# Attention and experts in one kernel: layer 0 routes each batch one pass sooner

## The chip, the cores and the metric

The kernel runs as one program on one core of a Trainium2 chip. A core has five engines, each with its own in-order queue: TensorE (PE, with its weight loads as PEld), VectorE (DVE), ScalarE (ACT), GpSimd (POOL) and SyncE (SP); they are held together by semaphores alone. The metric is the device time of one execution in microseconds (us). The kernel before took 808.4 us, the median of three runs (806.72, 808.40, 810.31).

## The reference

32 batches of 128 rows and 128 features pass through two layers; each block adds to the residual `x`. Only layer 0 is touched:

```
x = x + L0_xattn(layernorm(x), ctx, ctx)      # 16 heads of 8
x = x + L0_ffn(layernorm(x))                  # 8 experts, one per row
x = x + L1_xattn(layernorm(x), ctx, mask)     # not touched
x = x + L1_ffn(layernorm(x))                  # not touched

def L0_ffn(inputs):                           # cut to the routing
    num = inputs @ waff.T                     # 8 numbers per row
    aff = num / (norm(inputs) * norm(waff) + 1e-9)
    cap = clip(floor(S * sigmoid(aff.mean() - threshold)), 4, S)
    expert = argmax(aff)                      # "choice"
    keep   = rank of the row in its batch for that expert < cap
    out    = sum over experts of gelu(x_e @ W1_e + b1_e) @ W2_e + b2_e
```

The kernel sorts the rows by expert: it gives each row a place in a table in memory (`sorted_x`), scatters the rows there, and lets the experts work on tiles of 128 sorted rows.

## The kernel before

**Attention and routing interleaved.** Layer 0 runs 32 passes, one per batch `b`. All five engines run the same loop, written out by hand, and each queue's order is the order of the code. In pass `b` TensorE computes scores, exponent shifts, the values product and projections of neighbouring batches. VectorE takes maxima, normalises and makes the new residual of batch `b-1` (`residual`, L735) and, at the end of its pass, its mean and variance (`residual_stats`, L739 and L741, tile `stats`).

**The routing of a batch `r`** is a chain that runs through the passes that follow:
- GpSimd's loop index `r+2`: `route_norm` (L238 to L244) turns the variance into a scale and writes the normalised rows `xn2[r]`, which the trace calls `xy`. From r = 27 (`SCALED`) on, GpSimd only makes the scale and VectorE writes the rows (`route_scale`, L746).
- TensorE in pass `r+4`: `route_transpose` (L336) transposes `xn2[r]`, ScalarE copies it (`route_copy`, L533, tile `r_xnT`), and TensorE multiplies it with `waff` (`affinity`, L367). ScalarE's copy stands in its queue ahead of the pass's four exponentials (L552), which the values product needs.
- VectorE copies the eight numbers (`num_copy`, L628).

**Groups.** Batches are chosen in five groups: 0 to 7, 8 to 15, 16 to 23, 24 to 27 and 28 to 31. For a group GpSimd makes denominators (L253 to L263), VectorE chooses experts in ten small instructions (`choose`, L634 to L673), TensorE counts rows (`places`, L384 to L390) and VectorE turns counts into places (`locate`, L699 to L710, tile `r_pos_s`). Choices of groups 0 and 1 are already spread over five passes (`SPREAD = 2`); group 2 is chosen in one piece in pass 27, group 3 in pass 31, group 4 after the loop.

**Scatter.** GpSimd then sends each batch's rows to their places with one indirect DMA (`scatter`, L270): one in each of the passes 16 to 23, two in 24 to 27, none in 28, up to three from 29 on, and the rest after the loop. GpSimd's queue after the loop is: scale of batch 30, scatter of batch 24 (the first that needs group 3's places), scale of batch 31, denominators of group 4, scatters of batches 25 to 31. The experts' first tile is loaded once all 32 scatters have landed.

**The tail.** After pass 31 come, on TensorE, what is left of the routing (batches 28 to 31, two groups' places), the last output and sums over the experts' weights (`expert_sums_part`, L1003). `LATE = 28` says from which batch on the routing uses PSUM banks that the attention no longer needs.

Of the kernel before, what the change touches and what calls it, by code (L numbers as in the profile page):

```python
# [71 lines left out]
def attention_routing_block(nc, ctx, space, consts, x, ctxT, w, wr, x_res, xn2, stats2, psum, dram):  # L72
# [10 lines left out]
    SPREAD = 2  # L83
# [8 lines left out]
    LATE = 28  # L92
# [220 lines left out]
    def tensor_part(pe, expert_sums_part):  # L313
# [4 lines left out]
        def x_transpose(b, s):  # L318
            pe.wait_ge(xn_ready, b + 1)
            if b == 2:  # L320
                pe.wait_ge(v_ready, 2)
            elif 2 < b < 6:
                pe.wait_ge(qz_ready, b)
            wait(pe, rsem["num"], b - 5)
            nc.tensor.transpose(first_x(b), xn[:, s, :], ident[:]).then_inc(xt_done, 1)

        def route_transpose(r):
            pe.wait_ge(rsem["xn2"], r + 1)
            if r >= LATE:
                pe.wait_ge(mx_ready, 4 * B)  # L330
                pe.wait_ge(rsem["xnT"], r)
            else:
                pe.wait_ge(qz_ready, min(r + 6, B))
            if r == B - 5:
                pe.wait_ge(rsem["num"], r)
            nc.tensor.transpose(xnp[r >= LATE], xn2[:, r, :], ident[:]).then_inc(rsem["xnt"], 1)  # L336
# [23 lines left out]
        def affinity(r):  # L360
            pe.wait_ge(rsem["xnT"], r + 1)
            if r >= LATE:
                pe.wait_ge(mx_ready, 4 * B)
                pe.wait_ge(rsem["num"], r)
            elif r + 4 in close_at:
                pe.wait_ge(rsem["place"], 4 * close_at[r + 4] + 1)
            nc.tensor.matmul(nump[r >= LATE], rt["xnT"][:, r % 2, :], rt["waffT"][:], start=True, stop=True).then_inc(rsem["num_done"], 1)  # L367

        def places(q):
# [5 lines left out]
            if q < SPREAD:  # L375
                pe.wait_ge(rsem["xnT"], z + 4)
            elif z + 5 <= B:
                pe.wait_ge(rsem["xnT"], z + 1)
# [86 lines left out]
        for b in range(B):  # L465
# [4 lines left out]
            if b >= 4:  # L470
                route_transpose(b - 4)
# [4 lines left out]
            else:  # L476
                back_transposes(b - 1, 1 - s)
            minus_max(b, 1)
            if b >= 4:
                affinity(b - 4)  # L480
# [15 lines left out]
            else:  # L496
                route_transpose(B - 4)
        affinity(B - 4)
        back_transposes(B - 1, 1)
        route_transpose(B - 3)  # L500
        places(NG - 2)
# [14 lines left out]
    def scalar_part(act, after_exps):  # L516
# [57 lines left out]
        for b in range(B):  # L574
# [19 lines left out]
            if b >= 3:  # L594
                route_copy(b - 3)
# [5 lines left out]
    def vector_part(dve):  # L601
# [73 lines left out]
        def choose(q):  # L675
            choose_reciprocal(q)
            choose_affinity(q)
            choose_score(q)
            choose_expert(q)
            choose_seen(q)  # L680

# [79 lines left out]
        for b in range(B):  # L761
# [11 lines left out]
            if b >= 4:  # L773
                num_copy(b - 4)
# [7 lines left out]
            if b - 4 in group_at and SPREAD <= group_at[b - 4] < NG - 2:  # L782
                choose(group_at[b - 4])
# [9 lines left out]
            if b == B - 1:  # L793
                residual_stats(b - 1, 1 - s)
                route_scale(b - 2)
                choose(NG - 2)
# [4 lines left out]
        num_copy(B - 4)  # L801
        normalise(B - 1, 1)
        route_scale(B - 2)
        locate(NG - 2)
# [1774 lines left out]
```

## Time and profile before

| | before |
|---|---|
| median of three runs | 808.4 us |
| the profiled execution's own time | 806.13 us |
| its span, first to last instruction | 804.1 us |
| PE busy | 758.8 us, 94% |
| DVE busy | 673.9 us, 84% |
| POOL busy | 477.1 us, 59% |
| ACT busy | 439.8 us, 55% |
| mean granted clock of TensorE | 0.990 of full speed |

Times in the trace are counted from the first instruction. Layer 0 takes the time to about 218 us, the experts come next, and layer 1 follows. Shares of the whole span say little about the stage that the change touches: each stretch is to be read by itself. An idle time in brackets behind an instruction is that of its engine just before it, with the instruction that ended it. The changed kernel's line numbers are those of before up to about L500, then one less, and from about L680 on five more.

### The profile page before, as it was taken

To read this page: it belongs to the slowest core of one execution; us is meant where nothing else is said; L and a number is where in the kernel's file an instruction comes from. 1 tells how busy PE (TensorE), PEld (TensorE's weight loads), DVE (VectorE), ACT (ScalarE), POOL (GpSimd) and SP (SyncE) were. 2 spreads that over 40 slices of the span, in tenths; PEclk is the share of its full clock that TensorE was granted. 3 is DMA by queue.
4 is the path that set the end of the run, shared out by engine and by line. 5 is a ranking of instruction groups with operands and counts; after the bars stand their busy time and mean duration, and the time that the engine had idled before them with its cause. 6 is when DMAs were issued, how large, how long until landed. Compare 5 with 4: busy or idle time off the path is not lost.

```text
span 804.1 us, 28859 instructions
## 1 busy us (share of the span) xinstructions
PE 758.8 (94%) x10843; PEld 639.3 (80%) x10873; DVE 673.9 (84%) x1776; ACT 439.8 (55%) x1077; POOL 477.1 (59%) x914
## 2 busy tenths in 40 slices
PE   8999999998789999899999999999999999999973
PEld 6777777766689997788888888888888888888861
DVE  5888889887767765599999999999899999999876
ACT  3666666656066663545555555655545555555442
POOL 6758578888768664244654655646546555464334
PEclk9999999999999999999999999999999999999996
DMA  8986320000422211121131221221322313213120
GB/s 239 369 344 236 146 84 15 19 15 29 145 74 63 61 47 37 39 65 45 44 87 45 61 73 46 81 52 46 87 46 60 73 45 76 57 46 78 39 44 14
DMA packets 68253, 65.81 MB, mean 82 GB/s; under 512 B 23714, under 2 KB 49042, under 8 KB 68114
## 3 DMA queue, kind: packets, MB, share of 16 engines
q1 hardware_dynamic: 53250, 39.71, 18.6%
q10 hardware_dynamic: 12816, 20.06, 6.7%
q0 software_dynamic: 2048, 4.20, 1.8%
q8 instruction: 86, 1.41, 0.7%
q14 instruction: 53, 0.43, 0.2%
HBM read 35.89 MB, written 24.37 MB: 75 GB/s over the span
## 4 chain that ended last, share of the span: by engine, by line
PE 55%; DVE 19%; DMA 12%; issue 5%; SPq 4%; POOL 3%; ACT 1%; DVEq 1%; ACTq 0%; another core or an unknown queue 0%; POOLq 0%
DMA a_r_all<-a_r_rows 6%; DMA a_r_rows<-a_rT 4%; PE psum L432 4%; PE psum L1932 4%; PE psum L1042 4%; PE psum L1816 4%; PE psum L1864 4%; SPq L1481 3%; PE psum L1832 3%; PE psum L421 3%; PE psum L1845 3%; PE psum L1898 3%; PE psum L414 3%; PE psum L1030 3%; DVE a_mxf L2273 2%
## 5 line engine op out<-in xcount | busy, mean ns | idle before, releaser
L2114 ACT ACTIVATE a_pT<-psum 128x512 f32<-128x512 f32 x128 | 69.5, 594 | 49.0 <-PE psum L1919 34.0
L720 DVE TENSOR_REDUCE l_mx<-psum 128x4 bf16<-128x512 f32 x128 | 81.9, 682 | 3.5 <-PE psum L403 1.8
L1587 POOL TENSOR_TENSOR f_hd<-f_hmc,a_wmean 128x1 f32<-128x1 f32 x32 | 6.7, 210 | 130.1 <-DVE f_hr L2373 128.8
L2273 DVE TENSOR_REDUCE a_mxf<-psum 128x8 f32<-128x1024 f32 x64 | 77.5, 1211 | 3.1 <-PE psum L1888 3.1
L1832 PEld LDWEIGHTS psum<-a_cTm,a_Wk 128*128 128x128 f32 x512 | 64.2, 191 | 19.6 <-issue 19.6
L1816 PEld LDWEIGHTS psum<-a_xT,a_Wq 128*128 128x128 f32 x512 | 64.3, 192 | 14.2 <-issue 13.4
L552 ACT ACTIVATE l_pT<-psum 128x512 f32<-128x512 f32 x128 | 70.5, 597 | 7.8 <-PE psum L421 7.5
L1581 POOL TENSOR_SCALAR f_hq<-f_ht 128x512 bf16<-128x512 f32 x31 | 60.3, 1946 | 20.0 <-ACT f_ht L2158 19.9
L1898 PE MATMUL psum<-a_qT,a_kT 64*128 64x128 f32 x1024 | 71.0, 278 | 0.0
L1832 PE MATMUL psum<-a_cTm,a_Wk 128*128 128x128 f32 x512 | 70.1, 281 | 0.0
L1864 PE MATMUL psum<-a_Wv,a_cTm 128*128 128x512 f32 x128 | 69.8, 632 | 0.1
L1816 PE MATMUL psum<-a_xT,a_Wq 128*128 128x128 f32 x512 | 69.6, 279 | 0.0
L2158 ACT ACTIVATE f_ht<-f_h,f_big_m,f_hr 128x512 f32<-128x512 f32 x32 | 26.0, 814 | 77.6 <-DVE f_hr L2373 75.5
L1932 PE MATMUL psum<-a_pT,a_v 128*32 128x128 f32 x2048 | 62.7, 274 | 0.6 <-DVE a_oT L2298 0.6
L1845 PE MATMUL psum<-a_Wo,a_oT 128*128 128x128 f32 x512 | 62.6, 275 | 0.0
L1898 PEld LDWEIGHTS psum<-a_qT,a_kT 64*128 64x128 f32 x1024 | 62.1, 188 | 0.0
L1932 PEld LDWEIGHTS psum<-a_pT,a_v 128*32 128x32 f32 x2048 | 53.9, 110 | 8.7 <-issue 5.9
L1845 PEld LDWEIGHTS psum<-a_Wo,a_oT 128*128 128x128 f32 x512 | 59.7, 192 | 0.2 <-issue 0.2
L421 PEld LDWEIGHTS psum<-negI,l_mx 128*128 128x128 bf16 x512 | 34.9, 100 | 25.0 <-DVE l_mx L720 22.7
L2145 ACT COPY a_v<-psum 128x512 f32<-128x512 f32 x64 | 37.6, 588 | 21.3 <-PE psum L1864 21.3
L1103 ACT ACTIVATE e_hT<-psum,e_w1t 128x128 f32<-128x128 f32 x156 | 44.6, 369 | 6.4 <-issue 5.7
L2298 DVE TENSOR_TENSOR a_oT<-psum,a_r_all 128x512 f32<-128x512 f32 x64 | 41.7, 678 | 7.1 <-issue 4.5
(322 smaller groups left out, 2064.1 us busy)
## 6 DMA issues: line engine op xcount, KB each, us to landing
sorted_x<-r_zeros ACTq DMA_DIRECT2D x12, 1408.0 KB, 7.0
a_r_all<-a_r_rows SPq DMA_DIRECT2D x124, 128.0 KB
e_xt<-sorted_x SPq DMA_DIRECT2D x39, 64.0 KB, 1.8
sorted_y<-e_yt ACTq DMA_DIRECT2D x39, 64.0 KB, 1.6
e_w<-in_E_W1b SPq DMA_DIRECT2D x1, 2064.0 KB
a_cin<-in_ctx SPq DMA_DIRECT2D x32, 64.0 KB, 2.7
out<-f_x SPq DMA_DIRECT2D x32, 64.0 KB, 2.3
x_res<-in_x SPq DMA_DIRECT2D x1, 512.0 KB, 5.2
```

The source lines that it names most:

```text
L421: last = nc.tensor.matmul(tp[k][:, j * S:(j + 1) * S], mx[:, b % 2, h:h + 1].to_broadcast([P, P]), negI[:], start=False, stop=(j == Q4 - 1 ...
L552: nc.scalar.activation(pT[:, k, :], tp[k], ACT.Exp, scale=SCALE).then_inc(exp_ready, 1)
L720: nc.vector.tensor_reduce(mx[:, s, Q4 * k:Q4 * k + Q4], maxp[k % 2].rearrange("p (h t) -> p h t", h=Q4), AX_X, ALU.max).then_inc(mx_ready, 1)
L1581: nc.gpsimd.tensor_scalar(hq[:], ht[:], -M, 127.0, ALU.add, ALU.min).then_inc(hq_ready, 1)
L1816: last = nc.tensor.matmul(bank[:, i * S:(i + 1) * S], Wq[:, 4 * half + i, :], xT[:, b % 2, :], start=True, stop=True)
L1832: last = nc.tensor.matmul(bank[:, i * S:(i + 1) * S], Wk[:, 4 * half + i, :], context_of(b), start=True, stop=True)
L1845: last = nc.tensor.matmul(pa[:, 0:D], oT[:, p, :], Wo[:, p, :], start=(p == 0), stop=(p == NP - 1))
L1864: nc.tensor.matmul(bank, context_of(b), Wv[:, 512 * half:512 * half + 512], start=True, stop=True).then_inc(v_done, 1)
L1898: last = nc.tensor.matmul(tp[e][:, i * S:(i + 1) * S], keys_of(b)[r, p, :], qT[r, b % 2, p, :], start=(half == 0 and i == 0), stop=(half = ...
L1932: last = nc.tensor.matmul(op[half][32 * j:32 * j + 32, i * S:(i + 1) * S], values_of(b)[:, 8 * half + 4 * e + i, part], pT[:, 2 * half + e ...
L2114: nc.scalar.activation(pT[:, 2 * half + e, :], tp[e], ACT.Exp, scale=SCALE).then_inc(exp_ready, 1)
L2273: nc.vector.tensor_reduce(mxf[:, 8 * half:8 * half + 8].rearrange("p (e h) -> p e h", e=2), psum[:, 0:2, :].rearrange("p e (h t) -> p e h ...
```

## The change

Only layer 0's schedule changes. The arithmetic and the number of instructions on TensorE, VectorE and GpSimd stay as they are.
- `route_transpose`, `affinity`, `route_copy` and `num_copy` of batch `r` move from pass `r+4` to pass `r+3`. In passes 30 and 31, where VectorE writes the rows, the transpose stands behind the back transposes of the attention instead of ahead of them.
- Batch 28 is routed in pass 31, no longer after the loop, and `LATE` is 29.
- The choice of groups 2 and 3 is cut in two: `choose_first` (five instructions) in passes 26 and 30, `choose_second` (five) in passes 27 and 31.
- After the loop, group 3's counting stands first on TensorE, and its `locate` first on VectorE.

GpSimd's code is not changed.

```diff
-    LATE = 28
+    LATE = 29
...
-            wait(pe, rsem["num"], b - 5)
+            wait(pe, rsem["num"], b - 4)
             nc.tensor.transpose(first_x(b), xn[:, s, :], ident[:]).then_inc(xt_done, 1)
...
-                pe.wait_ge(qz_ready, min(r + 6, B))
-            if r == B - 5:
+                pe.wait_ge(qz_ready, min(r + 5, B))
+            if r >= B - 5:
                 pe.wait_ge(rsem["num"], r)
...
-            elif r + 4 in close_at:
-                pe.wait_ge(rsem["place"], 4 * close_at[r + 4] + 1)
+            elif r + 3 in close_at:
+                pe.wait_ge(rsem["place"], 4 * close_at[r + 3] + 1)
...
             if q < SPREAD:
-                pe.wait_ge(rsem["xnT"], z + 4)
+                pe.wait_ge(rsem["xnT"], z + 5)
             elif z + 5 <= B:
-                pe.wait_ge(rsem["xnT"], z + 1)
+                pe.wait_ge(rsem["xnT"], z + 2)
...
-            if b >= 4:
-                route_transpose(b - 4)
+            if 3 <= b < SCALED + 3:
+                route_transpose(b - 3)
             if b in close_at:
                 places(close_at[b])
             if b == 0:
                 expert_sums()
             else:
                 back_transposes(b - 1, 1 - s)
+            if b >= SCALED + 3:
+                route_transpose(b - 3)
             minus_max(b, 1)
-            if b >= 4:
-                affinity(b - 4)
+            if b >= 3:
+                affinity(b - 3)
...
-            else:
-                route_transpose(B - 4)
-        affinity(B - 4)
+        places(NG - 2)
         back_transposes(B - 1, 1)
         route_transpose(B - 3)
-        places(NG - 2)
         affinity(B - 3)
...
             pv_copy(b, s)
-            if b >= 3:
-                route_copy(b - 3)
+            if 2 <= b < B - 1:
+                route_copy(b - 2)
...
-        def choose(q):
+        def choose_first(q):
             choose_reciprocal(q)
             choose_affinity(q)
             choose_score(q)
+
+        def choose_second(q):
             choose_expert(q)
             choose_seen(q)
...
-            if b >= 4:
-                num_copy(b - 4)
+            if b >= 3:
+                num_copy(b - 3)
...
-            if b - 4 in group_at and SPREAD <= group_at[b - 4] < NG - 2:
-                choose(group_at[b - 4])
+            if b - 3 in group_at and SPREAD <= group_at[b - 3] < NG - 1:
+                choose_first(group_at[b - 3])
+            if b - 4 in group_at and SPREAD <= group_at[b - 4] < NG - 1:
+                choose_second(group_at[b - 4])
...
                 residual_stats(b - 1, 1 - s)
                 route_scale(b - 2)
-                choose(NG - 2)
...
-        num_copy(B - 4)
+        locate(NG - 2)
         normalise(B - 1, 1)
         route_scale(B - 2)
-        locate(NG - 2)
         num_copy(B - 3)
```

On VectorE, the choice of group 2 in pass 27 of the kernel before, from the residual to the next batch's queries (`l_qz`); `r_` tiles are the routing's:

```order
L735 TENSOR_TENSOR x_res<-psum,l_xb 128x128
L634 RECIPROCAL r_tmp<-r_den 128x64
L642 TENSOR_TENSOR r_aff<-r_num,r_tmp 128x64
L644 TENSOR_REDUCE r_mval<-r_aff 128x8
L651 TENSOR_TENSOR r_tmp<-r_aff,r_mval 128x64
L654 TENSOR_TENSOR r_score<-r_tmp,r_weight 128x64
L661 TENSOR_REDUCE r_smax<-r_score 128x8
L663 TENSOR_TENSOR r_tcrb<-r_score,r_smax 128x64
L669 TENSOR_TENSOR r_tcr<-r_score,r_smax 128x64
L671 TENSOR_REDUCE r_gsum<-r_tcr 128x8
L673 TENSOR_TENSOR r_seen<-r_seen,r_gsum 128x8
L622 SCALAR_TENSOR_TENSOR l_qz<-psum,l_bq,group_rows 128x512
```

The same place of VectorE in the changed kernel, now in pass 26:

```order
L740 TENSOR_TENSOR x_res<-psum,l_xb 128x128
L633 RECIPROCAL r_tmp<-r_den 128x64
L641 TENSOR_TENSOR r_aff<-r_num,r_tmp 128x64
L643 TENSOR_REDUCE r_mval<-r_aff 128x8
L650 TENSOR_TENSOR r_tmp<-r_aff,r_mval 128x64
L653 TENSOR_TENSOR r_score<-r_tmp,r_weight 128x64
L621 SCALAR_TENSOR_TENSOR l_qz<-psum,l_bq,group_rows 128x512
```

The other five instructions stand at the same place of pass 27, between `x_res` and `l_qz`; group 3 is cut in the same way in passes 30 and 31.

On TensorE, from the values product of pass 31 (L432) into the tail, in the kernel before; L336 and L367 are routing, L385 to L390 group 3's places, L439 and L444 the attention's last transposes:

```order
L432 MATMUL psum<-l_pT,l_v 32x128 x16
L336 MATMUL psum<-ident,xy 128x128
L367 MATMUL psum<-r_waffT,r_xnT 128x8
L439 MATMUL psum<-ident,l_oev 128x128 x4
L336 MATMUL psum<-ident,xy 128x128
L385 MATMUL psum<-r_tcrb,r_before_t 128x32
L388 MATMUL psum<-r_tcrb,r_ones_b 128x24
L388 MATMUL psum<-r_tcrb,r_ones_b 128x16
L388 MATMUL psum<-r_tcrb,r_ones_b 128x8
L390 MATMUL psum<-r_seen,r_ones_b 128x32
L367 MATMUL psum<-r_waffT,r_xnT 128x8
L444 MATMUL psum<-ident,l_on 128x128
```

The same stretch of TensorE in the changed kernel:

```order
L432 MATMUL psum<-l_pT,l_v 32x128 x16
L385 MATMUL psum<-r_tcrb,r_before_t 128x32
L388 MATMUL psum<-r_tcrb,r_ones_b 128x24
L388 MATMUL psum<-r_tcrb,r_ones_b 128x16
L388 MATMUL psum<-r_tcrb,r_ones_b 128x8
L390 MATMUL psum<-r_seen,r_ones_b 128x32
L439 MATMUL psum<-ident,l_oev 128x128 x4
L336 MATMUL psum<-ident,xy 128x128
L367 MATMUL psum<-r_waffT,r_xnT 128x8
L444 MATMUL psum<-ident,l_on 128x128
```

One transpose and one affinity (batch 28) are gone from between the values product and the back transposes, and the places stand in front.

On TensorE in pass 31, around the first and second exponent shifts (L421), in the kernel before:

```order
L414 MATMUL psum<-l_qz,l_kT 128x512 x4
L421 MATMUL psum<-negI,l_mx 128x128 x4
L336 MATMUL psum<-ident,xy 128x128
L439 MATMUL psum<-ident,l_oev 128x128 x4
L421 MATMUL psum<-negI,l_mx 128x128 x4
L367 MATMUL psum<-r_waffT,r_xnT 128x8
```

The same in the changed kernel; pass 30 reads alike:

```order
L414 MATMUL psum<-l_qz,l_kT 128x512 x4
L421 MATMUL psum<-negI,l_mx 128x128 x4
L439 MATMUL psum<-ident,l_oev 128x128 x4
L336 MATMUL psum<-ident,xy 128x128
L421 MATMUL psum<-negI,l_mx 128x128 x4
L367 MATMUL psum<-r_waffT,r_xnT 128x8
```

The transpose, now of batch 28 instead of 27, has moved behind the back transposes.

## Rows read from the trace of the kernel before

**Rows 1.** Windows, passes 25 and 28: us, engines' busy time, clock, DMA share, GB/s.

```profile
156.11:161.87 5.76, 5.74 (x90) 4.44 (x90) 4.81 (x13) 3.81 (x10) 4.95 (x8) 1.00 0.07 23
173.38:181.59 8.21, 6.34 (x98) 4.74 (x98) 7.49 (x25) 3.89 (x10) 7.13 (x11) 1.00 0.05 16
```

**Rows 2.** Waits of POOL, 153.6 to 218.1 us: total us, times, longest.

```profile
POOL r_vpe L238 <- DVE stats L741: 0.5, 1, 0.5
```

**Rows 3.** Timeline of POOL in the tail: start us, length, line, tiles, [idle before].

```profile
204.43 1.08 POOL L270 DMA_INDIRECT sorted_x<-xy,r_pos_s  x1 [1.42 <-DVE r_pos_s L710]
205.55 0.25 POOL L238 TENSOR_SCALAR r_vpe<-stats 128x1 f32<-128x1 f32 x1
```

**Rows 4.** Timeline of DVE, the statistics of batch 31.

```profile
204.77 0.18 DVE L741 BATCH_NORM_AGGREGATE stats<-l_bn 128x2 f32<-128x6 f32 x1
```

**Rows 5.** Timeline of PE, the route transposes of passes 27, 28 and 29.

```profile
170.12 0.28 PE L336 MATMUL psum<-ident,xy 128*128 128x128 f32 x1
...
176.97 0.30 PE L336 MATMUL psum<-ident,xy 128*128 128x128 f32 x1 [0.93 <-DVE l_qz L622]
...
184.09 0.28 PE L336 MATMUL psum<-ident,xy 128*128 128x128 f32 x1
```

**Rows 6.** Timeline of POOL, normalised rows of batches 24 to 26, scale of 27.

```profile
171.21 0.81 POOL L244 TENSOR_SCALAR xy<-x_res,stats,r_rs 128x128 f32<-128x128 f32 x1
...
177.76 0.81 POOL L244 TENSOR_SCALAR xy<-x_res,stats,r_rs 128x128 f32<-128x128 f32 x1
...
184.30 0.81 POOL L244 TENSOR_SCALAR xy<-x_res,stats,r_rs 128x128 f32<-128x128 f32 x1
...
185.52 0.22 POOL L238 TENSOR_SCALAR r_vpe<-stats 128x1 f32<-128x1 f32 x1
```

**Rows 7.** Timeline of DVE, passes 26 and 27: queries, and the choice of group 2.

```profile
168.26 0.75 DVE L622 SCALAR_TENSOR_TENSOR l_qz<-psum,l_bq,group_rows 128x512 f32<-128x512 f32 x1 [0.69 <-PE psum L351]
...
173.24 0.55 DVE L634 RECIPROCAL r_tmp<-r_den 128x64 f32<-128x64 f32 x1
...
176.09 0.74 DVE L622 SCALAR_TENSOR_TENSOR l_qz<-psum,l_bq,group_rows 128x512 f32<-128x512 f32 x1
```

**Rows 8.** Timeline of DVE: statistics of batch 27, rows of batch 27.

```profile
184.57 0.18 DVE L741 BATCH_NORM_AGGREGATE stats<-l_bn 128x2 f32<-128x6 f32 x1
...
190.34 0.33 DVE L746 TENSOR_SCALAR xy<-x_res,stats,r_rs 128x128 f32<-128x128 f32 x1
```

**Rows 9.** Timeline of POOL beside the choice of group 2: a scatter.

```profile
173.96 1.07 POOL L270 DMA_INDIRECT sorted_x<-xy,r_pos_s  x1 [0.17 <-issue]
```

**Rows 10.** Timeline of PE, the route transpose of pass 30.

```profile
189.76 0.28 PE L336 MATMUL psum<-ident,xy 128*128 128x128 f32 x1
```

**Rows 11.** Timeline of ACT: copy of a transpose in pass 30; last attention copy.

```profile
190.08 0.27 ACT L533 COPY r_xnT<-psum 128x128 f32<-128x128 f32 x1 [1.08 <-PE psum L336]
...
199.86 0.57 ACT L557 COPY l_oev<-psum 128x512 f32<-128x512 f32 x1
```

**Rows 12.** Timeline of PE, back transposes of batch 31.

```profile
200.89 0.63 PE L439 MATMUL psum<-ident,l_oev 128*128 128x128 f32 x4
```

**Rows 13.** Timeline of DVE: residual of batch 30, normalisation and residual of batch 31.

```profile
197.95 0.29 DVE L735 TENSOR_TENSOR x_res<-psum,l_xb 128x128 f32<-128x128 f32 x1 [1.19 <-PE psum L450]
...
202.00 0.25 DVE L726 RECIPROCAL l_rden<-psum 128x16 f32<-128x16 f32 x1
...
204.12 0.28 DVE L735 TENSOR_TENSOR x_res<-psum,l_xb 128x128 f32<-128x128 f32 x1
```

**Rows 14.** Windows, columns as in rows 1: the kernel's end, the start of the experts.

```profile
788.00:792.00 4.00, 0.86 (x3) 0.22 (x3) 3.62 (x14) 1.77 (x3) 1.84 (x6) 0.59 0.00 0
218.10:223.43 5.33, 2.71 (x7) 0.90 (x5) 5.26 (x6) 0.27 (x1) 5.33 (x6) 1.00 0.13 40
```

**Rows 15.** Groups by line on PE, 785 to 804.1 us: busy us, mean ns.

```profile
L1981 PE MATMUL psum<-f_wq,f_xqT 128*128 128x512 bf16 x2 | 1.1, 545 | 0.0
```

**Rows 16.** The same group of PE, 400 to 785 us.

```profile
L1981 PE MATMUL psum<-f_wq,f_xqT 128*128 128x512 bf16 x27 | 10.2, 379 | 0.8 <-ACT a_v L2145 0.7 <-issue 0.2
```

More of the change, by code:

```diff
@@ L678, in choose @@
             choose_score(q)
+        def choose_second(q):
             choose_expert(q)
             choose_seen(q)
+        def choose(q):
+            choose_first(q)
+            choose_second(q)
         def choose_spread(q, part):
```

## The prediction

> **What bounds the kernel now.** I read the shares of the engines first, then the windows of layer 0, then who waits in its last third, and last the timelines of that third. Over the whole span TensorE is nearly always busy, and so it is in layer 0's loop: a pass takes 5.76 us and holds 5.74 us of matmuls [rows 1]. The reader should stop at the second of these windows. Pass 28 takes 8.21 us with 6.34 of matmuls, so something else decides there.
>
> Two engines share the last third. GpSimd, at 59% of the span an unlikely candidate, has almost no rest from 153.6 us to the end of its scatters at about 218: the table of its waits has one of 0.5 us on statistics [rows 2] and one of 1.42 us, in the tail, ahead of the scatter of batch 24, which stood ready and waited for group 3's places [rows 3]. From 205.55 on, where it scales batch 31, it only works off its own queue: denominators, then seven scatters; nothing that TensorE or VectorE do later than the statistics of batch 31 ends that chain. So the end of layer 0 is the start of that one instruction (L238 at 205.55) plus a fixed rest, and every edit is to be priced by what it does to that start. It has two possible releasers: GpSimd's own queue, which decided before, and the statistics of batch 31, ready at 204.77 + 0.18 = 204.95 [rows 4].
>
> **Passes 3 to 26.** Transpose, copy, affinity and number copy are the same instructions one batch on, at the same place of the pass. They cost nothing as long as the rows of batch r are there a pass sooner. GpSimd's rows are early while it scatters at most once a pass; I take the cost as nothing. The same instructions no longer follow the values product of pass 31.
>
> **Pass 27: a new wait.** From pass 24 on GpSimd scatters twice a pass and falls behind. In pass 27 TensorE's L336 started at 170.12 [rows 5] with batch 23; now batch 24 stands there, whose rows GpSimd finishes at 171.21 + 0.81 = 172.02 [rows 6]. TensorE waits 1.90 us. Behind it in TensorE's queue stand the back transposes and the rest of the pass, and ScalarE's copy stands ahead of the exponentials, so the whole pass moves by 1.90; GpSimd doesn't, since it works off a backlog.
>
> **Passes 28 and 29.** Batch 25 is ready at 177.76 + 0.81 = 178.57, against 176.97 before: 1.60 late. The wait isn't added to the one before, since the releaser is the same GpSimd, which kept its times. The 0.93 us that TensorE waited there for `l_qz` [rows 5] are swallowed by it. Batch 26 is ready at 185.11, and TensorE now comes at 184.09 + 1.60 = 185.69: no wait. Delay so far 1.60.
>
> The split of the choice doesn't pay beyond that. It took 176.09 - 173.24 = 2.85 us in pass 27 [rows 7] and held `l_qz` and with it the transpose of pass 28. Half of it now lies in pass 26, where VectorE rested 0.69 us ahead of `l_qz` [rows 7]; some 0.8 us stick out and end in pass 27, beside the 1.90 us for which TensorE waits for GpSimd. The other half falls under the wait in pass 28. If that cover went, the 0.8 would be paid.
>
> GpSimd itself is now held once: it scaled batch 27 at 185.52 [rows 6] and its statistics were ready at 184.57 + 0.18 = 184.75 [rows 8]; 1.60 later is 186.35, so it waits 0.83 us. That is less than the 1.42 us of rest that it had in the tail.
>
> The first half of the choice now runs ahead of GpSimd's rows of batch 24 instead of behind them. The trace has a scatter beside the choice with 1.07 us [rows 9], and one in the tail with 1.08 [rows 3]: no sign that the one slows the other, so I take nothing. The Trainium skill, "SBUF — State Buffer", section "Who interferes with whom", says that a VectorE instruction with two inputs in SBUF and a GpSimd instruction that reads SBUF take turns. By that page three such instructions of about 0.2 us each could make batch 24 some 0.6 us later, and the forecast would be about 0.6 us higher; the scatter's two rows speak against it.
>
> **Passes 30 and 31.** Here VectorE writes the rows at the end of its pass. Those of batch 27 are done at 190.34 + 0.33 = 190.67 [rows 8], and L336 of pass 30 started at 189.76 [rows 10]: 0.91 us too early. ScalarE's copy (at 190.08, 0.32 after L336 [rows 11]) is late by the same, and the exponentials behind it too; the back transposes that now go first fill TensorE's wait, not ScalarE's. Both ends: nothing if the back transposes (0.63 [rows 12]) covered TensorE and ScalarE's own slack the rest, 1.2 with the copy's 0.27 on top. I take 0.91, the difference of the two rows, for each of the two passes. Delay at the residual of batch 30: 1.60 + 2 x 0.91 = 3.42 us, 197.95 [rows 13] becomes 201.37. Group 3's first half lies in VectorE's wait of pass 30, the second (under 2.85 / 2 = 1.4 us) behind that residual while TensorE does the values product, so it only delays the scale of batch 30, which has room.
>
> **The tail.** Before, the back transposes of batch 31 started at 200.89 [rows 12], behind batch 28's affinity. That is gone, and what is late next is ScalarE's copy, done at 199.86 + 0.57 = 200.43 [rows 11]; + 3.42 gives 203.85, so they are 2.96 late. Before, VectorE took them up at 202.00 [rows 13] though they were done at 200.89 + 0.63 = 201.52, since the choice of group 3 and a number copy stood ahead. Those 0.48 us are gained: the group's places are found while ScalarE still copies. 2.96 - 0.48 = 2.48, so the statistics of batch 31 come at 204.95 + 2.48 = 207.43. The residual at 204.12 [rows 13] stood behind four small instructions of `locate`, which may give another 0.3; I leave it.
>
> GpSimd by itself would be there sooner. The scatter of batch 24 needs no wait of 1.42 any more, but it lost 0.83: 205.55 + 0.83 - 1.42 = 204.96. So the statistics decide: the scale of batch 31 starts at 207.43 instead of 205.55, **1.9 us later**, with GpSimd resting some 2.5 us ahead of it. All behind it keeps its distances, as group 4's choice follows GpSimd's denominators. The experts and layer 1 have the same code and start 1.9 us later.
>
> Against the profiled execution's own 806.13 us that is 808.0. The median of the three runs is 2.3 us above that execution, so on the scale of the runs it is 808.4 + 1.9 = **810.3**. That is 0.2%. A measurement of this kernel can tell about 0.5%, 4 us, from no change, so the forecast is no change that shows, on the slow side. With the bounds above (passes 30 and 31 between 0 and 1.2 each, 0.3 in the tail, 0.6 for the port) the mechanism itself gives 810.3 - 2.1 = 808.2 to 810.3 + 1.2 = 811.5.
>
> **Rivals.** *The tail gains and nothing is lost (807.0).* If TensorE reached batch 31 without the new waits, its statistics would come at 204.95 - 0.94 (the 3.42 - 2.48 that the tail saves) = 204.01, ahead of GpSimd, which then closes its whole rest of 1.42 us: 808.4 - 1.4. More can't be won, since GpSimd has no other rest. For it: the 1.42 us are real, and what pass 28 lost (8.21 - 5.76) is larger than any one new wait. Against it: rows 5 and 6 hold the transposes to GpSimd's times, whatever else is faster.
>
> *The waits add up (813.2, slower).* This takes GpSimd being held by TensorE already in passes 27 and 28, so that its rows keep their distance behind. Then the price is 1.90 in pass 27, 1.60 in 28, 185.11 - 184.09 = 1.02 in 29 and 0.91 twice, 6.34, less 0.94 in the tail: statistics at 204.95 + 5.40 = 210.35, 4.8 us after 205.55, and 808.4 + 4.8. It decides from the point where statistics come later than GpSimd asks for them. In pass 29 that is 0.77 us away [rows 6, 8], for it; in the passes before, GpSimd has a backlog and asked late [rows 2], against it.
>
> *TensorE's clock falls (820).* The new waits give TensorE rests of up to 1.9 us. The granted clock is 1.00 (2.4 GHz) in a window with only 2.71 us of matmuls in 5.33, and 0.59 in one with 0.86 in 4.00 [rows 14]; passes 27 to 31 hold 5.7 in some 7.7, so by the rows it stays. If it fell to 1.2 GHz, a 512-column matmul takes 545 ns [rows 15] instead of 379 [rows 16], 44% more: 5.74 x 0.44 = 2.5 us a pass, 10 for the four that follow. The Trainium skill, "TensorE: Matmul & The Clock Gate", section "Part 1: The HAM clock gate", says that the clock of a TensorE that rests is halved until it has worked again. By that page alone a longer rest would bring this rival about; this trace agrees for the kernel's end and shows none in layer 0.
>
> **How the numbers follow.** Forecast 0.72, gain 0.17, adding up 0.08, clock 0.03. The three runs lie from 1.7 below to 1.9 above their median. The low end is the gain's 807.0 less 1.7, the high end the forecast's own upper bound, 811.5, plus 1.9: 805.3 to 813.4, which also holds the middle of the waits that add up. Faster by over 0.5% (under 804.4) takes the gain and more luck than the three runs show: 0.04. Slower by over 0.5% (over 812.4) has the clock, more than half of the adding up, and a high run of the forecast: 0.12. The rest, 0.84, is no change.
>
> **What would show it.** In the trace of the changed kernel: L336 of pass 27 idle some 1.9 us ahead of it with GpSimd's L244 as releaser, L336 of pass 28 at about 178.6, and that of 29 without a wait; one wait of GpSimd for statistics near 186; about half a microsecond at L336 of passes 30 and 31 with VectorE's `xy` as releaser and ScalarE's copy 0.9 late; no wait of a scatter for `r_pos_s` in the tail, but one of about 2 us of L238 for the statistics of batch 31; last scatter's end near 220. Wrong would be: transposes of passes 27 and 28 that don't wait, batch 31 scaled before 205.5, GpSimd's rows of batches 24 and 25 moved by more than 0.3 us, or a difference that arises behind the experts' first tile.

## The result and the profile after

The changed kernel takes 810.77 us, the kernel before 808.14 us, medians of 22 runs each; the ratio is 1.0033 with a 95% interval of 1.0017 to 1.0048. That is +2.6 us: slower, and by less than the 0.5% that the prediction called "no change". The profiled execution of the changed kernel has a span of 806.7 us (before 804.1).

Single runs lie up to some 5 us to either side of their median, so I read the stage that the change touches by itself. I take it from the start of the values product (L432) of pass 25 to the end of the last scatter: 56.21 us before (161.87 to 218.08), 60.62 us after (160.89 to 221.51), 4.4 us more. Windows of the changed kernel, one for each of the passes 26 to 31, then the tail up to GpSimd's scale of batch 31, then the rest up to the last scatter. Columns as in [rows 1]; the last three are granted clock, DMA share and GB/s.

```profile
160.89:166.65 5.76, 5.75 (x90) 4.44 (x90) 4.86 (x14) 3.81 (x10) 4.84 (x10) 1.00 0.01 3
166.65:176.29 9.64, 7.84 (x89) 6.20 (x89) 6.97 (x22) 4.03 (x10) 8.25 (x14) 0.77 0.09 29
176.29:184.72 8.43, 7.23 (x100) 5.49 (x99) 5.82 (x17) 3.90 (x10) 6.96 (x12) 0.86 0.05 16
184.72:190.38 5.66, 5.66 (x90) 4.42 (x89) 4.51 (x11) 3.80 (x11) 2.42 (x5) 1.00 0.02 6
190.38:196.82 6.44, 5.49 (x83) 3.69 (x82) 4.81 (x13) 3.74 (x10) 5.04 (x9) 1.00 0.10 33
196.82:203.38 6.56, 5.14 (x74) 3.38 (x74) 4.14 (x15) 2.96 (x8) 5.31 (x7) 1.00 0.09 30
203.38:209.00 5.62, 4.08 (x58) 3.35 (x59) 3.72 (x19) 2.85 (x7) 2.92 (x5) 1.00 0.12 38
209.00:221.51 12.51, 9.95 (x86) 9.17 (x85) 8.42 (x37) 0.27 (x1) 9.79 (x14) 1.00 0.73 207
```

Read it by differences from before, whose lengths in the same order were 5.75, 5.76, 8.21, 5.68, 5.52, 5.50, 7.26 and 12.53: pass 27 loses 3.88, pass 28 0.22, passes 30 and 31 0.92 and 1.06, the tail gives back 1.64. The second thing to see is the clock: 0.77 and 0.86 in passes 27 and 28, where the kernel before had 1.00.

TensorE's route transposes of passes 27 to 31, which answer to [rows 5, 10]:

```profile
171.10 0.33 PE L336 MATMUL psum<-ident,xy 128*128 128x128 f32 x1 [1.79 <-POOL xy L244]
179.85 0.28 PE L336 MATMUL psum<-ident,xy 128*128 128x128 f32 x1
187.21 0.28 PE L336 MATMUL psum<-ident,xy 128*128 128x128 f32 x1
193.84 0.33 PE L336 MATMUL psum<-ident,xy 128*128 128x128 f32 x1 [0.36 <-DVE xy L751]
200.68 0.33 PE L336 MATMUL psum<-ident,xy 128*128 128x128 f32 x1 [0.75 <-DVE xy L751]
```

GpSimd, to be held against [rows 2, 3, 6]: the rows of batch 25, the scale of batch 27, the scatter of batch 24, the scale of batch 31.

```profile
176.78 0.81 POOL L244 TENSOR_SCALAR xy<-x_res,stats,r_rs 128x128 f32<-128x128 f32 x1
...
187.96 0.23 POOL L238 TENSOR_SCALAR r_vpe<-stats 128x1 f32<-128x1 f32 x1 [2.91 <-DVE stats L746]
...
205.90 1.08 POOL L270 DMA_INDIRECT sorted_x<-xy,r_pos_s  x1 [0.25 <-DVE r_pos_s L715]
...
209.00 0.22 POOL L238 TENSOR_SCALAR r_vpe<-stats 128x1 f32<-128x1 f32 x1 [2.02 <-DVE stats L746]
```

GpSimd kept its times: the rows of batch 25 are done 16.70 us after the start of the stage in both kernels. The scatter's wait of 1.42 us is gone, and GpSimd rests 2.02 us for the statistics of batch 31 instead, as forecast. What was not forecast starts at 171, in windows of one microsecond of the same kernel:

```profile
169.00:170.00 1.00, 0.30 (x4) 0.13 (x3) 1.00 (x3) 0.00 (x0) 0.83 (x3) 1.00 0.25 82
170.00:171.00 1.00, 0.00 (x0) 0.00 (x0) 0.32 (x2) 0.00 (x0) 0.89 (x2) 1.00 0.00 0
171.00:172.00 1.00, 0.90 (x10) 0.89 (x10) 0.10 (x1) 0.54 (x2) 0.81 (x4) 0.91 0.00 0
172.00:173.00 1.00, 1.00 (x12) 0.79 (x10) 0.84 (x5) 0.82 (x2) 0.82 (x2) 0.50 0.00 0
...
178.00:179.00 1.00, 1.00 (x21) 0.70 (x16) 0.20 (x1) 0.58 (x1) 0.89 (x2) 0.67 0.00 0
```

TensorE (first busy column) rests from 169.3 to 171.1, and just after it has started again the granted clock falls to 0.50, the level of 1.2 GHz, and stays there to about 178.7 although TensorE is busy throughout.

### The profile page after: what moved, and what is told of

Its sections match the earlier page's. It is cut to its first block, busy times and chain, and to the rows that moved or that the text cites. A ratio compares the mean times of both kernels' runs of the same rounds, so it can differ in the third digit from the quotient of the medians.

```text
span 806.7 us, 28891 instructions
## 1 busy us (share of the span) xinstructions
PE 765.1 (95%) x10873; PEld 640.5 (79%) x10873; DVE 673.6 (84%) x1776; ACT 439.8 (55%) x1077; POOL 477.0 (59%) x914
## 3 DMA queue, kind: packets, MB, share of 16 engines
q8 instruction: 86, 1.41, 0.7%
## 4 chain that ended last, share of the span: by engine, by line
PE 55%; DVE 19%; DMA 12%; issue 5%; SPq 4%; POOL 4%; ACT 1%; DVEq 1%; ACTq 0%; POOLq 0%
DMA a_r_all<-a_r_rows 6%; PE psum L1047 4%; PE psum L1937 4%; DMA a_r_rows<-a_rT 4%; PE psum L1821 4%; PE psum L432 4%; PE psum L1837 4%; SPq L1486 4%; PE psum L1869 4%; PE psum L1850 3%; PE psum L1035 3%; PE psum L1903 3%; PE psum L421 3%; PE psum L414 3%; DVE a_mxf L2278 2%
## 5 line engine op out<-in xcount | busy, mean ns | idle before, releaser
L421 PEld LDWEIGHTS psum<-negI,l_mx 128*128 128x128 bf16 x512 | 35.4, 100 | 25.0 <-DVE l_mx L725 23.5
```

Of the source, the lines that this page charges most:

```text
L421: last = nc.tensor.matmul(tp[k][:, j * S:(j + 1) * S], mx[:, b % 2, h:h + 1].to_broadcast([P, P]), negI[:], start=False, stop=(j == Q4 - 1 ...
```

## The experiments

The theory after the result: the doubled scatters ahead of batch 24's rows make TensorE wait 1.8 us in pass 27; that rest lets the clock fall; passes 30 and 31 lose by VectorE's late rows. The rivals: the loss is the wait alone, the clock's fall is chance, or it comes from elsewhere (the halved choice, the experts).

**1. Even scatters: take away what makes TensorE wait.**

```diff
-            for _ in range(1 if b < 24 else 2 if b < 29 else 3):
+            for _ in range(1 if b < 26 else 2 if b < 29 else 3):
```

> The changed kernel, with GpSimd's scatters spread otherwise: one a pass up to pass 25, two in 26 to 28, three after (before: two in 24 to 27, none in 28). The same scatters in all, so by pass 29 GpSimd is where it was. Theory (late rows of batch 24 in pass 27 cost a wait, and the wait costs TensorE's clock): rows of batch 24 come some 2.5 us sooner, L336 of passes 27 and 28 doesn't wait, the granted clock stays 1.00 there, and the time falls by 1.9 + 2.1 = 4.0 us against the changed kernel, so it is 806 to 807.5, at or under the kernel before. Rival (the loss is in passes 30 and 31 and the tail, and the wait of pass 27 is only taken from a later one): under 1 us better than the changed kernel, 810.

Measured: ratio to before 0.9982 (0.9951 to 1.0013). Passes 27 and 28 and the last scatters of this kernel:

```profile
166.22:172.32 6.10, 5.80 (x89) 4.43 (x89) 5.86 (x19) 3.81 (x10) 5.15 (x9) 1.00 0.07 24
172.32:179.75 7.43, 6.37 (x98) 4.75 (x98) 6.13 (x20) 3.89 (x10) 6.52 (x11) 1.00 0.05 18
...
203.70:216.21 12.51, 10.94 (x89) 9.65 (x88) 8.42 (x37) 0.27 (x1) 9.79 (x14) 1.00 0.82 213
```

The wait in pass 27 is gone, the clock stays at 1.00, and the two passes take 13.53 us instead of 18.07, the stage 55.75 instead of 60.62. So the doubled scatters are the origin of what passes 27 and 28 lose, 4.54 of the 4.87 us. Passes 30 and 31 stay long (6.44 and 6.20). The ratio is 0.5%, 4.1 us, under the changed kernel's, as the theory wanted; experiment 10 finds half of that.

**2. Keep the wait, fill the rest.** TensorE multiplies the identity with itself while GpSimd's rows are on their way.

```diff
+            if b == 27:
+                pe.wait_ge(oev_ready, b)
+                for _ in range(14):
+                    nc.tensor.matmul(yp[:, 0:S], ident[:], ident[:], start=True, stop=True)
             if 3 <= b < SCALED + 3:
```

> The changed kernel with 14 matmuls of ident with ident in pass 27 ahead of the route transpose, into a bank that the next transposes overwrite (their result is used by nothing): TensorE works while it waits. Theory (the clock falls because TensorE rests): the transpose starts as late as in the changed kernel, within 0.2 us, but the clock stays 1.00 in passes 27 and 28, and the time falls by about 2 us against the changed kernel, to some 808.7. Rival (the clock fell in the one profiled execution only, or for another reason): the time stays at 810.8, and the clock falls here too or fell in no other execution.

Measured: ratio 1.0036 (1.0004 to 1.0067), stage 58.66 us. Passes 27 and 28:

```profile
166.16:175.09 8.93, 8.91 (x117) 7.61 (x118) 5.98 (x19) 3.81 (x10) 7.63 (x12) 1.00 0.07 24
175.09:182.26 7.17, 6.16 (x98) 4.71 (x99) 6.10 (x20) 3.90 (x10) 6.21 (x12) 1.00 0.09 29
```

The fillers run over: the transpose starts 5.67 us into the pass, after 4.45 in the changed kernel, so the wait even grew by 1.22 us. Yet the clock stays at 1.00 and the two passes take 16.10 us instead of 18.07. So some 2.0 us of the loss are the clock's, at the least, if it is the fillers that kept it: this is one execution, while in all the other profiles with that wait the clock fell in pass 27 or 28. Without it the two passes take between 14.88 (16.10 - 1.22) and 16.10, an estimate of 0.9 to 2.1 us over before's 13.97; the forecast said 1.60. The theory's 2 us didn't show in the whole time (1.0036, the changed kernel 1.0033): behind the last scatter this execution took 590.1 us, the changed kernel 585.2.

**3. GpSimd writes the rows of batches 27 and 28 too.**

```diff
-    SCALED = 27
+    SCALED = 29
```

> The changed kernel with SCALED = 29: GpSimd writes the rows of batches 27 and 28 as well, VectorE those of 29 to 31 only, and the transposes of passes 30 and 31 stand ahead of the back transposes again. Theory (passes 30 and 31 lose 0.9 to 1.1 us each since VectorE writes the rows too late): both waits for VectorE's xy go, passes 30 and 31 take some 5.6 us instead of 6.5, GpSimd's 2 x 0.81 us more lie in its rests; 1.5 to 2 us better than the changed kernel, 809. Rival (GpSimd is the bound in the tail): the two rows make it 1.6 us later there, 810.8 or more.

Measured: ratio 1.0002 (0.9976 to 1.0028), stage 59.53 us. TensorE waits 1.78 us in pass 27. Passes 30, 31 and the two parts of the tail:

```profile
188.48:194.00 5.52, 5.06 (x83) 3.67 (x82) 4.56 (x12) 3.72 (x10) 4.27 (x7) 1.00 0.08 27
194.00:199.77 5.77, 4.99 (x74) 3.48 (x75) 3.64 (x14) 3.08 (x8) 4.68 (x8) 1.00 0.07 23
199.77:206.76 6.99, 4.45 (x51) 3.27 (x52) 4.10 (x19) 2.90 (x7) 6.05 (x9) 0.78 0.12 40
206.76:220.29 13.53, 12.48 (x92) 11.70 (x92) 7.83 (x36) 0.27 (x1) 9.70 (x15) 0.86 0.72 201
```

Passes 30 and 31 are 0.92 and 0.79 us shorter than in the changed kernel: VectorE's rows made them long. Passes 27 and 28 keep the same wait, and the clock falls there again (16.28 us together). But the gain doesn't reach the end: the tail takes 20.52 us instead of 18.13, with the clock down. GpSimd scaled batch 31 without a wait, so its own queue was the bound there, as the rival said.

**4. The wait alone, in the kernel before.**

```diff
+            if b == 27:
+                pe.wait_ge(rsem["xn2"], 25)
             if b >= 4:
                 route_transpose(b - 4)
```

> The kernel before with one wait more and nothing else: TensorE in pass 27 waits for the rows of batch 24, as the changed kernel does, though it transposes batch 23. Theory (this one wait and the clock after it make the loss): L336 of pass 27 starts some 1.9 us late, the clock falls to 0.50 for 5 to 7 us behind it, TensorE is 2.5 to 3 us late in pass 29, and the statistics of batch 31 come so much later than GpSimd wants them: 809.5 to 811, as slow as the changed kernel. Rival (GpSimd's 1.42 us of rest and pass 28's 2.4 us of slack hide it): 808.1, no change.

Measured: ratio 1.0016 (0.9991 to 1.0042), stage 60.17 us. The transpose of pass 27, then passes 27 and 28:

```profile
170.27 0.33 PE L336 MATMUL psum<-ident,xy 128*128 128x128 f32 x1 [1.79 <-POOL xy L244]
```

```profile
165.83:173.59 7.76, 5.96 (x90) 4.47 (x90) 4.87 (x14) 3.81 (x10) 6.48 (x11) 1.00 0.06 19
173.59:183.45 9.86, 7.85 (x99) 6.09 (x99) 7.63 (x25) 4.04 (x10) 8.76 (x15) 0.83 0.09 28
```

One wait of 1.79 us put into the kernel before costs its stage 3.96 us against the first profile of before. Of these, 2.00 are the wait's, in pass 27 at full clock. The clock falls in pass 28, behind a second rest (1.08 us, `l_qz`), and that pass takes 9.86 us instead of 8.21. It falls once more in the tail, and the last part takes 0.93 us more:

```profile
206.78:220.24 13.46, 12.43 (x90) 11.63 (x89) 7.83 (x36) 0.27 (x1) 9.72 (x15) 0.85 0.67 202
```

Such falls come without the added wait too. The second profile of the kernel before (experiment 9) has as much time at half clock in its stage, 10.2 us by windows of a quarter microsecond, though not all in the same places; against that one the wait costs 60.17 - 58.27 = 1.90 us. The whole time decides nothing here: its interval holds both the theory's loss and the rival's "no change".

**5. Even scatters and GpSimd's rows together**, the candidate that should have beaten both: the edits of 1 and 3.

> The changed kernel with the scatters held to one a pass until pass 26 (as in the experiment with even scatters) and, besides, GpSimd writing the normalised rows of batches 27 and 28 as well (SCALED = 29). Theory (each wait of TensorE in passes 27, 30 and 31 has its own releaser, and two edits remove them all): passes 27 to 31 take about 6.1, 7.4, 5.7, 5.5 and 5.6 us, against 6.10, 7.43, 5.69, 6.44 and 6.20 with even scatters alone; if the tail keeps its 5.6 + 12.5 us, the last scatter ends 54.2 us after the values of pass 25, 2.0 us before the kernel before (56.2), and the ratio of the times is 0.995 to 0.999. Rival (the rows written on GpSimd only push its scatters into the tail, and TensorE's clock falls there as it did when the rows alone were moved): the tail takes 20 to 20.5 us instead of 18.1, the stage ends at 56.2 and the ratio is 0.999 to 1.002.

Measured: ratio 1.0012 (0.9989 to 1.0034), stage 57.34 us. Passes 27 to 30 are as hoped (6.10, 7.43, 5.67, 5.52), but pass 31 takes 8.42 at a clock of 0.80. TensorE and GpSimd there:

```profile
195.64 0.33 PE L336 MATMUL psum<-ident,xy 128*128 128x128 f32 x1 [1.76 <-POOL xy L244]
```

```profile
192.25 0.96 POOL L270 DMA_INDIRECT sorted_x<-xy,r_pos_s  x1 [0.30 <-issue]
...
194.77 0.81 POOL L244 TENSOR_SCALAR xy<-x_res,stats,r_rs 128x128 f32<-128x128 f32 x1
```

Neither theory held: three scatters (at 189.56, 190.98 and 192.25) stand ahead of batch 28's rows, and the wait of pass 27 has come back four passes later, clock included.

**6. Even scatters, the choice whole again.**

```diff
-                choose_first(group_at[b - 3])
...
-                choose_second(group_at[b - 4])
+                choose(group_at[b - 4])
```

> The changed kernel with even scatters, and the choice of the third and fourth group whole in one pass again (four passes behind, as in the kernel before), not halved. Theory (the halving moves work that VectorE has room for): every pass within 0.3 us of the run with even scatters, the last scatter at 55.75 +- 0.5 us after the values of pass 25. Rival (the halving pays, since with routing a pass sooner VectorE's queue is full in the pass in which a group closes): pass 28, where the whole choice then stands, is 0.8 us longer or more (8.2 against 7.4) and the end is later by as much.

Measured: ratio 1.0014 (0.9990 to 1.0037), stage 58.73 us. Passes 27 and 28 take 5.75 and 8.37, together 14.12 us against 13.53 in experiment 1: the halving pays 0.59 us. Pass 28 alone is 0.94 us longer, as the rival said, and its transpose shows why:

```profile
175.81 0.30 PE L336 MATMUL psum<-ident,xy 128*128 128x128 f32 x1 [1.09 <-DVE l_qz L621]
```

The tail up to the scale of batch 31 takes 6.57 us instead of 5.62, at a clock of 0.84.

**7. Even scatters in the kernel before.** The edit of 1 with 26 in place of 24, nothing else.

> The kernel before with the scatters held to one a pass until pass 26, nothing else. Theory (in the kernel before GpSimd's rows are asked for a pass later and its doubled scatters of passes 24 and 25 lie under that slack): passes 27 to 31 within 0.2 us of the kernel before (5.76, 8.21, 5.68, 5.52, 5.50), the end within 0.3 us of 56.2 but for what the clock does in the tail, ratio 1.000 +- 0.002. Rival (even scatters are worth something by themselves, so that the gain of the changed kernel with even scatters is not the change's): pass 28 drops from 8.21 to 7.4, the end to 55.4 or sooner, ratio 0.998 or less.

Measured: ratio 0.9997 (0.9976 to 1.0019), stage 57.44 us. Pass 27 takes 5.76, pass 28 9.42 at a clock of 0.82. So even scatters by themselves show no gain, neither in pass 27 nor in the time. The surprise is the clock: TensorE waits in pass 28 for the same tile as in the kernel before (1.07 us for `l_qz`, before 0.93), and this time the clock fell, there and in the tail.

**8. The changed kernel again, twice, unaltered.**

> The changed kernel, unaltered, once more with a profile on another chip. Theory (the wait of 1.8 us in pass 27 is what takes TensorE's clock down, and does so whenever the kernel runs): TensorE waits 1.7 to 1.9 us for GpSimd's rows in pass 27, the granted clock of pass 27 is 0.75 to 0.9, and passes 27 and 28 together take 17.5 to 18.5 us. Rival (the fall of the clock was a chance of that one execution): the same wait, a clock of 1.00, and passes 27 and 28 together take 16.0 to 16.4 us.

> The changed kernel, unaltered, a third time. Theory (the wait for GpSimd's rows in pass 27 is the same in every execution, the fall of the clock that follows is not): TensorE waits 1.75 to 1.9 us in pass 27; the stage takes 58 to 58.4 us if the clock stays at 1.00 in all passes and 59.5 to 60.8 us if it falls in pass 27 or 28. Rival (the clock falls in every execution of this order): it falls in pass 27 or 28 here too.

Measured: stages of 59.67 and 59.56 us. TensorE waited 1.83 and 1.79 us in pass 27, but that pass kept its full clock both times; the clock fell in pass 28. Passes 27 and 28 of the third execution (the second: 7.79 and 9.31), then its transpose of pass 28:

```profile
165.81:173.57 7.76, 5.95 (x90) 4.48 (x90) 5.97 (x19) 3.81 (x10) 6.48 (x11) 1.00 0.06 19
173.57:182.81 9.24, 7.81 (x99) 6.09 (x99) 6.00 (x20) 4.03 (x10) 8.14 (x14) 0.82 0.09 30
```

```profile
176.79 0.33 PE L336 MATMUL psum<-ident,xy 128*128 128x128 f32 x1 [0.57 <-POOL xy L244]
```

Their sums, 17.10 and 17.00, are under the 17.5 that the theory allowed and over the rival's 16.4. The clock fell in all three executions, as the rival of the second repeat said, but not in the same place. The transpose shows what the first profile hid: where pass 27 keeps its clock, TensorE comes to pass 28 early enough to wait for GpSimd again, as forecast.

**9. The kernel before again, unaltered.**

> The kernel before, unaltered, once more with a profile on another chip. Theory (whether a rest of TensorE of 1 to 2 us is followed by half clock differs from one execution to the next, and the kernel before has such rests in pass 28 and in the tail): TensorE waits in the same places for the same lengths within 0.2 us, but the clock falls in pass 28 or in the tail, and the stage takes 57 to 58 us instead of 56.2. Rival (its rests are too short for that): clock 1.00 in all of these passes and in the tail to the scale of batch 31, 56.2 +- 0.3 us.

Measured: a stage of 58.27 us, 2.06 more than in the first profile. TensorE's waits in pass 28 first, of the first profile and of this one:

```profile
176.97 0.30 PE L336 MATMUL psum<-ident,xy 128*128 128x128 f32 x1 [0.93 <-DVE l_qz L622]
177.83 0.19 PE L385 MATMUL psum<-r_tcrb,r_before_t 128*128 128x64 bf16 x1 [0.56 <-ACT r_xnT L533]
```

```profile
175.03 0.30 PE L336 MATMUL psum<-ident,xy 128*128 128x128 f32 x1 [0.95 <-DVE l_qz L622]
175.89 0.19 PE L385 MATMUL psum<-r_tcrb,r_before_t 128*128 128x64 bf16 x1 [0.56 <-ACT r_xnT L533]
```

And the windows around them, again the first profile and then this one:

```profile
176.00:177.00 1.00, 0.07 (x2) 0.06 (x1) 1.00 (x3) 0.00 (x0) 0.97 (x3) 1.00 0.16 57
177.00:178.00 1.00, 0.44 (x8) 0.28 (x9) 1.00 (x3) 0.69 (x2) 0.81 (x2) 1.00 0.03 8
178.00:179.00 1.00, 1.00 (x19) 0.99 (x15) 0.90 (x6) 0.12 (x2) 0.92 (x3) 1.00 0.00 0
```

```profile
174.00:175.00 1.00, 0.09 (x2) 0.00 (x0) 1.00 (x3) 0.00 (x0) 0.98 (x3) 1.00 0.12 41
175.00:176.00 1.00, 0.41 (x6) 0.28 (x7) 1.00 (x2) 0.63 (x2) 0.81 (x3) 1.00 0.08 25
176.00:177.00 1.00, 1.00 (x19) 0.99 (x17) 0.90 (x6) 0.14 (x1) 0.92 (x3) 0.94 0.00 0
177.00:178.00 1.00, 0.96 (x11) 0.68 (x11) 0.93 (x6) 0.60 (x1) 0.89 (x2) 0.50 0.00 0
...
182.00:183.00 1.00, 1.00 (x24) 0.59 (x12) 0.62 (x1) 0.00 (x0) 0.89 (x2) 0.50 0.00 0
```

The same program, the same waits to 0.02 us, nearly the same busy shares, and once the clock stays at 1.00, once it is 0.50 from 177 to 183 and again for 3.4 us in the tail. So the profile on which the prediction rests showed the lucky one of two outcomes.

**10. Even scatters again**, to see whether they beat the kernel before.

> The changed kernel with even scatters once more, on another chip, since the first comparison (0.9982, 0.9951 to 1.0013) left open whether it beats the kernel before. Theory (the stage is 0.5 to 2 us shorter than the kernel before, the more so where TensorE's clock falls in that kernel and not here): the last scatter 55.5 to 56.0 us after the values of pass 25, clock 1.00 throughout, ratio 0.997 to 0.9995. Rival (the first look was a lucky execution, and the clock falls in the tail here too, as in the run with the whole choice): the stage takes 57 us or more, ratio 1.000 to 1.002.

Measured: ratio 1.0008 (0.9991 to 1.0026), stage 55.73 us, each pass within 0.02 us of experiment 1. They don't: the two ratios lie on both sides of 1. Weighted by their intervals they make 1.0002 +- 0.0015, an estimate; the changed kernel's 1.0033 +- 0.0016 lies 0.0031 +- 0.0022 above it. So holding the scatters back takes the loss out of the time as well, and gains nothing beyond it. The stage is the shortest of all, 0.5 to 2.5 us shorter than the kernel before, and the time doesn't show it.

**11. The changed kernel with the choice whole**, its scatters as they are (the edit of 6).

> The changed kernel with its doubled scatters from pass 24 as they are, and the choice of the third and fourth group whole again. Theory of the prediction (TensorE is late in pass 28 by GpSimd's rows in any case, so that the halving pays nothing): passes 27 and 28 together within 0.5 us of the changed kernel at like clock, which is 15.4 to 16.4 us where the granted clock stays 1.00 and 17 to 18.1 us where it falls. Rival (it pays as it did beside even scatters, 0.6 us, because VectorE's late quotient l_qz is one more wait): TensorE waits some 1 us for l_qz in pass 28, and the two passes take 0.6 us or more beyond that.

Measured: stage 61.91 us. Passes 27 and 28 and the tail up to the scale of batch 31:

```profile
166.41:176.18 9.77, 7.98 (x89) 6.34 (x90) 5.86 (x16) 4.03 (x10) 8.39 (x14) 0.76 0.09 29
176.18:184.54 8.36, 7.09 (x99) 5.36 (x99) 7.10 (x23) 3.89 (x10) 6.89 (x12) 0.87 0.05 18
...
203.21:209.88 6.67, 5.20 (x53) 4.09 (x54) 4.73 (x24) 2.85 (x7) 2.90 (x5) 0.68 0.10 32
```

The two passes take 18.13 us, the changed kernel 18.07 with the clock down in the same place: under GpSimd's rows the halving pays nothing, as the prediction said, and the transpose of pass 28 waits for nothing. But the tail takes 1.05 us more, as it took 0.95 more in experiment 6. How much of that is the choice of group 3 and how much the clock (0.68 and 0.84) isn't separated.

**Where the rest of the time goes.** From the last scatter to the end the kernel before takes 586.0 and 588.3 us in its two profiles, the changed kernel 585.2, 585.4 and 585.4, even scatters 590.9 and 588.2; over all fourteen profiles it is 584.8 to 591.2. So what a stage gains can be lost behind it. In experiment 10 the clock fell right behind the last scatter, as the experts' first tile began, and was 0.50 from 222 to 225:

```profile
222.00:223.00 1.00, 1.00 (x7) 1.00 (x6) 1.00 (x2) 0.00 (x0) 0.11 (x1) 0.50 0.24 66
```

In layer 1 VectorE's exponent shifts (`a_mx`) are late more often: from 312 to 785 us TensorE waits for them 3 times in the changed kernel's first profile, 1.3 us in all, and 8 times, 3.1 us, in experiment 1. It does so 3 and 6 times in the two profiles of before, 4 and 3 times in the repeats of the changed kernel, 7 times in experiment 10. Why layer 1, whose code is the same, falls into one or the other stays open; no run was made for it.

## Why the prediction was right, and where not

- **The result.** +1.9 us was forecast, 2.6 us measured (1.4 to 3.9 by the interval), in the likeliest case. That the two lie so near is in part luck: the forecast left out the clock, which fell in all three profiles of the changed kernel and in one of the two of before, and it left out the spread of the parts behind the stage. At a clock of 1.00 in both kernels, experiment 2 puts the changed stage between 57.44 (58.66 - 1.22) and 58.66 us, an estimate of 1.2 to 2.5 us over before's 56.21; the 1.9 lies in it.
- **The wait of pass 27**: 1.90 forecast, 1.79, 1.83 and 1.79 measured in three executions, with the releaser named. Experiment 4 puts the same wait into the kernel before and finds 2.00 us in the pass; experiment 1 takes its origin away. The 0.6 us allowed for the port were not paid: GpSimd's rows of batch 24 are done 10.15 us after the start of the stage in both kernels.
- **Passes 27 and 28 together**: +1.60 forecast, because the second wait isn't added and swallows that for `l_qz`. The repeats, in which pass 27 kept its clock, bear this out up to the transpose of pass 28, which comes 16.79 and 16.75 us after the start of the stage, before 15.10: 1.69 and 1.65 late, by GpSimd's rows. For both passes without the clock the estimate is +0.9 to +2.1 (experiment 2). With it, +4.10, +3.13 and +3.03 against the first profile of before. The term had the right mechanism and left out the clock.
- **Passes 30 and 31**: 0.91 each forecast, 0.92 and 1.06 measured, and experiment 3 shows the cause. TensorE's part is the wait of 0.36 and 0.75. ScalarE's copy, which stands ahead of the exponentials, comes 1.02 and 1.41 us later in its pass than before, and the exponentials start right behind it:

```profile
194.21 0.27 ACT L532 COPY r_xnT<-psum 128x128 f32<-128x128 f32 x1 [2.09 <-PE psum L336]
...
201.04 0.27 ACT L532 COPY r_xnT<-psum 128x128 f32<-128x128 f32 x1 [2.49 <-PE psum L336]
```

- **The tail**: the delay of 3.42 at the residual of batch 30 was to become 1.9 at the scale of batch 31, 1.5 given back; measured 1.64. GpSimd rests 2.02 ahead of it (2.5 forecast) and no longer for `r_pos_s` of group 3 (1.42 before, 0.25 after). "All behind it keeps its distances" held here (12.53 before, 12.51 after), but not where the clock fell in the tail: in experiment 3 that part takes 13.53 us, as one of its scatters waits 1.41 us for group 4's places.
- **GpSimd held in pass 29**: 0.83 forecast, 2.91 measured in the first profile and 2.36 in the third. The step is right and its input, the delay of 1.60, was too small: pass 28 ended 4.11 and 3.05 us late, the clock's part included.
- **"The split of the choice doesn't pay beyond that"**: right under the cover that was named (experiment 11), and 0.59 us where the cover is gone (experiment 6), against the 0.8 forecast for that case. In the tail the prediction took 0.48 us for VectorE's earlier choice of group 3. With the choice whole the tail is 1.05 and 0.95 us longer, but the fallen clock comes with it in both experiments, so what the split is worth there stays open.
- **The step that failed**, though the time came out in the range, is "so by the rows it stays", of the clock, with a chance of 0.03. The row that I leaned on, 1.00 with 2.71 us of work in 5.33 [rows 14], was one outcome of several. The price was too high as well: in passes 27 and 28 the clock was down for 3.4 to 6.8 us and cost some 2 us where it was longest (experiment 2), not 10. The two profiles of the kernel before differ in whether it falls at all. The Trainium skill, "TensorE: Matmul & The Clock Gate", section "Part 1: The HAM clock gate", says that the window by which the clock is set runs free and doesn't start anew with a kernel, so that the point at which the clock rises varies from run to run. It says so of the rise alone; the profiles here show that a fall varies too (1.00 and 0.50 behind the same waits in experiment 9).
- **"The experts and layer 1 ... start 1.9 us later"** and else the same: not so. What lies behind the last scatter varies by up to 2.7 us between executions of one kernel, which no row of one profile could show, and it was 0.6 to 3.1 us shorter in the changed kernel's three profiles than in the two of before. That is a difference behind the experts' first tile, one of the prediction's own signs of being wrong; whether it comes of the change or of chance stays open.

With all clocks as they fell, the changed kernel's three stages have a mean of 59.95 us, the two of before 57.24: a difference of 2.7 us. That it is so near to the 2.6 us of the medians shows little: the same five executions differ by only 0.5 us in their whole time (means of 807.8 and 807.4 us), since the parts behind the stage vary by as much.

## What to carry to other kernels

When a step is asked for one pass sooner, look at what its producer has taken on ahead of it: here two scatters a pass, harmless before, became a wait of 1.8 us, and holding them to one a pass for two passes longer took it away (13.53 us for the two passes instead of 18.07). A wait on TensorE has a second price, the clock after it, which one profile can show or hide; take two profiles of the kernel before, and price the wait with and without it. A stage that gets 5 us shorter isn't a kernel that gets 5 us shorter, until the time says so.

## What the runs showed of the hardware

- A rest of TensorE of 1 to 2 us was followed by half clock in some executions and not in others of the same program (experiments 8 and 9). The clock was down for 6.8 us behind the wait of pass 27 in the changed kernel's first profile, and for 3.4 us in pass 28 of its repeats.
- With fillers that do no useful work the clock stayed at 1.00 in the one profile of experiment 2 and two passes were 2.0 us shorter, although the wait was longer. The whole time showed no gain.
